# Attention on Trainium2: the product of y with the reciprocal denominators moved from GpSimd to VectorE

## The chip, the core and the metric

The kernel runs on one core of a Trainium2 chip. Its time is the device time of the execution in microseconds (us); a median of several runs is given. The engines are named as in the profile: PE (TensorE, matrix products), PEld (its weight loads), DVE (VectorE), ACT (ScalarE), POOL (GpSimd) and SP (SyncE, which here only issues DMAs).

## What is computed

One transformer layer with adaptive layer norm on 2048 tokens of width 1024. The part that matters is the attention, with 32 query heads that share 8 key and value heads:

```python
q = (x @ Wq.T).reshape(b, t, h_kv, g, d).transpose(0, 2, 3, 1, 4)   # h_kv 8, g 4, d 32
k = (x @ Wk.T).reshape(b, t, h_kv, d).transpose(0, 2, 1, 3)
v = (x @ Wv.T).reshape(b, t, h_kv, d).transpose(0, 2, 1, 3)
att = jnp.einsum('bhgqd,bhkd->bhgqk', q, k) / scale
att = jax.nn.softmax(att, axis=-1)
y = jnp.einsum('bhgqk,bhkd->bhgqd', att, v)
return y.transpose(0, 3, 1, 2, 4).reshape(b, t, e) @ Wo.T + bo
```

In front of it stand the modulation, a layer norm and the products for q, k and v; behind it the output projection and a gated feed-forward network of 2752 inner columns. All of it is in float32 or in float32 split into two parts.

## The kernel before

The program has five stages. The attention stage (`stage_attention`) works in 32 units: 8 key heads times 4 blocks of 512 queries, with the 4 query heads of the group side by side. Each unit has 16 steps, `k` = 0 to 15, one for 128 keys. The order of every engine is written out by hand, and the engines meet through semaphores alone.

In a unit `u`, PE makes for each step four transposed score tiles (128 keys x 512 queries, `scores_t`), from which ACT takes the exponentials (`pr`, eight buffers, L1057). It also makes four "turns": score tiles (128 queries x 512 keys, `turn`) of a unit ahead, from which DVE takes maxima (L1086). A unit has 64 turns. They run ahead of their unit, so that the turns 60 to 63 of unit `u + 1` are made in step 12 of unit `u`, and those of unit `u + 2` follow from step 13 on. When all 64 are there, DVE forms the row maximum (`row_max`, L1091, end of step 12), PE transposes it in step 14 (L1160), DVE writes it as two rows (`max_rows`, L1099 and L1101, between turns 5 and 6), and SP stores these into the q stack (`store_max`, L907). The first `scores_t` of the next unit waits for that store. The turns and the transposition take four PSUM banks in rotation (`score_banks`), so PE can fill a bank only when DVE is through with the fourth tile back. In even steps PE also makes the products with v for two steps at once (`by_v`, 16 products).

The softmax denominators are sums of the exponentials. POOL adds them in pairs (`pair`, L996, eight in a unit, `j` = 0 to 7), with one further sum (`quad_sum`, L1009) and four sums by accumulating DMA (`sum_by_dma`, L1005, behind the pairs 1, 3, 4 and 7). Before it issues the third of these it waits for the first two. In the next unit PE finishes the sums by products with ones in steps 2, 4 and 6 (`denominators`), ACT copies the result in step 6 (`copy_den`, L1048), and it goes the way of `den_trip` on SP's queue: out to DRAM (L916), back in spread over 128 partitions (L919), through DVE's `recip` (L1106, in step 9 behind the step's second turn), out again (L927), and back as four loads, each of which spreads one row over 32 partitions of `rden_b` (L931, `rden_loaded`). Before these loads SP waits that the product of the unit before is done (`y_done`).

The product itself is `y_out` on POOL (L1016): `yo = ysb * rden_b`, 128 x 512 float32, all three in SBUF. `ysb` is ACT's copy of the accumulated y of the last unit (L1042, step 0). In a unit `u` POOL makes it for unit `u - 1`, behind pair 5 and the quad sum (`Y_AFTER`). SP stores the result with `store_y` (L850), which stands in its queue behind `store_max`; the loads of q for a later unit (L890) follow it. DVE runs the units 0 to 30 only; unit 31 has no turns. The last unit's product is `last_division` (L882) on DVE.

Of the kernel before, what the change touches and what calls it, by code (L numbers as in the profile page):

```python
# [7 lines left out]
ALU = mybir.AluOpType  # L8
# [11 lines left out]
GH = HQ // HKV  # L20
# [633 lines left out]
def stage_attention(nc, ctx, block, qkv, wo, q_dram, k_dram, v_dram, y_dram, den_dram, kq0, qs, vg, q_loaded, v_loaded,  # L654
# [9 lines left out]
    NU = HKV * QB  # L664
# [19 lines left out]
    DEN_COPY = 6  # L684
    RECIP_AT = 9
    Y_AFTER = 5
    DW = GH * NB // P
    TSTEP = 14
    PER = NTURN // KT
# [2 lines left out]
    with ExitStack() as st:  # L692
        def sb(name, shape, dt, offset):
            return place(nc, offset, "att_" + name, shape, dt)

        def sem(name):
            return ctx.enter_context(nc.semaphore("att_" + name))
# [6 lines left out]
        rden_b = sb("rden_rows", [P, NB], F32, offs[0])  # L704
# [3 lines left out]
        mT = [sb(f"max_T_{n}", [GH * NB // P, P], F32R, offs[6 + i]) for i, n in enumerate(("hi", "lo"))]  # L708
        den_in = sb("den_spread", [P, DW], F32, offs[8])
        rden = sb("rden_spread", [P, DW], F32, offs[9])  # L710
        ysb = [sb(f"y_raw{i}", [P, NB], F32, R5 + i * 4 * NB) for i in range(2)]
        yo = [sb(f"y_out{i}", [P, NB], F32, R5 + (2 + i) * 4 * NB) for i in range(2)]
# [13 lines left out]
        y_copied, y_done, y_stored = sem("y_copied"), sem("y_done"), sem("y_stored")  # L726
        const_done = sem("consts_done")
        den_copied, den_stored, den_loaded = sem("den_copied"), sem("den_stored"), sem("den_loaded")
        rden_stored, rden_loaded = sem("rden_stored"), sem("rden_loaded")
# [29 lines left out]
        def units(eng, unit):  # L759


            for u in range(NU):
                unit(u, u % BODY, u // QB)

        def is_first(u):
            return isinstance(u, int) and u == 0
# [5 lines left out]
        def nth_turn(u, q):  # L772
            return u * NT1 + event(q)

        def nth_transpose(u):
            return (u + 1) * NT1 + (0 if beyond(u, 1) else TQ)
# [36 lines left out]
        def turn_buffer(u, q):  # L813
            return smp[of_event[nth_turn(u, q)][0]]
# [17 lines left out]
        def steps_done(u, q):  # L832

            return 2 if u == 1 and q == TQ - 1 else 1

        def beyond(u, n):

            return isinstance(u, int) and u + n >= NU
# [46 lines left out]
        def _(sp):  # L885
# [24 lines left out]
            def spread(v):  # L910
                return v.rearrange("h (a w) -> (h a) w", w=DW)

# [60 lines left out]
        @block.gpsimd  # L973
        def _(pool):
            def pair(u, j):
                pool.wait_ge(exp_done, NST + 2 * GH * (j + 1) + u * NX)

                if j == 0:
                    pool.wait_ge(den_done, 1 + u * ND)
                elif j == 1:  # L980
                    if u:
                        pool.wait_ge(quad_done, u)
                elif j == 2:
                    if u:
                        pool.wait_ge(dma_sum[3], u * 16)
                elif j == 3:
                    pool.wait_ge(den_done, 3 + u * ND)
                elif j == 4:
                    pool.wait_ge(den_done, 2 + u * ND)
                elif j == 5:  # L990
                    pool.wait_ge(dma_sum[0], 16 + u * 16)
                elif j == 6:
                    pool.wait_ge(dma_sum[1], 16 + u * 16)
                elif j == 7:
                    pool.wait_ge(dma_sum[2], 16 + u * 16)
                nc.gpsimd.tensor_tensor(ps[PAIR_SLOT[j]][:], pr[2 * j % NP][:], pr[(2 * j + 1) % NP][:],  # L996
                                        ALU.add).then_inc(pair_done, 1)

            def sum_by_dma(u, i):
                into, other = DMA_SUM[i]  # L1000
                pool.wait_ge(pair_done, NP // 2 + SUM_PAIRS[i] + 1 + u * PAIRS)
                if i == 2:
                    pool.wait_ge(dma_sum[0], 16 + u * 16)
                    pool.wait_ge(dma_sum[1], 16 + u * 16)
                pool.dma_start(ps[into][:], ps[other][:], accum_op=ALU.add).then_inc(dma_sum[i], 16)  # L1005

            def quad_sum(u):
                pool.wait_ge(pair_done, NP // 2 + 6 + u * PAIRS)
                nc.gpsimd.tensor_tensor(ps[4][:], ps[4][:], ps[1][:], ALU.add).then_inc(quad_done, 1)  # L1009

            def y_out(u, c):

                pool.wait_ge(rden_loaded, 16 * GH + u * 16 * GH)
                pool.wait_ge(y_copied, u + 1)
                pool.wait_ge(y_stored, 16 + u * 16)
                nc.gpsimd.tensor_tensor(yo[c % 2][:], ysb[c % 2][:], rden_b[:], ALU.mult).then_inc(y_done, 1)  # L1016

            def unit(u, c, g):
                if is_first(u):
                    for i in range(2):  # L1020
                        pool.wait_ge(qkv["stored"][i], qkv["all_stored"])
                for j in range(PAIRS):
                    pair(u, j)
                    if j in DMA_AFTER:
                        sum_by_dma(u, DMA_AFTER[j])
                    if j == QUAD_AFTER:
                        quad_sum(u)
                    if j == Y_AFTER and not is_first(u):
                        y_out(u - 1, c - 1)

            pool.sem_inc(pair_done, NP // 2)
            nc.gpsimd.memset(ks[1][SR:SR + 2, :].bitcast(F32), -1.0).then_inc(const_done, 1)
            pool.wait_ge(const_done, 2)
            units(pool, unit)
# [46 lines left out]
        @block.vector  # L1081
        def _(v):
            def turn(u, c, q):

                v.wait_ge(sm_ready, nth_turn(u, q) + 1)
                nc.vector.reduce_max(cmax[c % 2][:, q:q + 1], turn_buffer(u, q)[:], AX.X  # L1086
                                     ).then_inc(sm_done, steps_done(u, q))

            def row_max(u, c):
                v.wait_ge(sm_done, nth_turn(u, NTURN - 1) + 1 + NSM)  # L1090
                nc.vector.reduce_max(rmax[c % 2][:], cmax[c % 2][:].rearrange("p (r k) -> p r k", k=T // NB),  # L1091
                                     AX.X).then_inc(rmax_done, 1)

            def max_rows(u, c):

                src = transpose_buffer(u)
                v.wait_ge(sm_ready, nth_transpose(u) + 1)
                v.wait_ge(m_stored, u * 32)
                nc.vector.tensor_copy(mT[0][:], src).then_inc(mT_hi, 1)  # L1099
                v.wait_ge(mT_hi, u + 1)  # L1100
                nc.vector.tensor_tensor(mT[1][:], src, mT[0][:].bitcast(F32), ALU.subtract).then_inc(sm_done, 1)  # L1101

            def recip(u):
                v.wait_ge(den_loaded, 16 + u * 16)
                v.wait_ge(rden_stored, 16 + u * 16)
                nc.vector.reciprocal(rden[:], den_in[:]).then_inc(rden_done, 1)  # L1106

            def first_y():
                v.wait_ge(wo.y_copied, 1)
                v.wait_ge(*first_y_room)  # L1110
                v.wait_ge(pv_done, NP + (NU - 1) * KT + KT // 2 + 2)
                raw = wo.y_first[:].rearrange("p (k t) -> p k t", t=P)
                nc.vector.tensor_copy(wo.ysp[0][0], raw).then_inc(wo.y0_hi, 1)
                v.wait_ge(wo.y0_hi, 1)
                nc.vector.tensor_tensor(wo.ysp[0][1], raw, wo.ysp[0][0].bitcast(F32), ALU.subtract).then_inc(wo.y_split, 1)  # L1115

            def unit(u, c, g):
                for k in range(KT):
                    ahead = turns(u, k)
                    if k == TSTEP and not ahead and not beyond(u, 1):  # L1120
                        max_rows(u + 1, c + 1)
                    for i, (n, q) in enumerate(ahead):
                        if n == 2 and q == TQ:
                            max_rows(u + 1, c + 1)
                        turn(u + n, c + n, q)
                        if i == 1 and k == RECIP_AT and not is_first(u):
                            recip(u - 1)
                    if k == TSTEP - 2 and not beyond(u, 1):
                        row_max(u + 1, c + 1)

            nc.vector.memset(ones[:], 1.0).then_inc(const_done, 1)
            v.sem_inc(sm_done, NSM + NT1)
            v.sem_inc(rmax_done, 1)
            v.sem_inc(mT_hi, 1)
            v.sem_inc(y_done, 2)
            v.sem_inc(y_stored, 16)
            for u in range(NU - 1):
                unit(u, u % BODY, u // QB)
            recip(NU - 2)
            first_y()  # L1140
            wo.lo_of_y(v, 1)
# [1055 lines left out]
```

## Time and profile before

| what | value |
|---|---|
| median of 3 runs | 3423.8 us (3422.91 to 3424.23) |
| the profiled execution's own time | 3422.06 us |
| its span in the trace | 3420.3 us |
| granted TensorE clock, mean | 0.995 |
| busy: PE, DVE, ACT, POOL | 98%, 66%, 46%, 48% of the span |
| attention stage | from about 400 to 1965 us |

The profile is of one execution. A row of a timeline gives the start in us from the span's start, the length, the engine ("q" behind it: an instruction of its queue, a DMA's issue), the line, what is written from what, the count of instructions merged into the row, and in brackets the idle time before it with what ended it. Lines are those of the kernel before. Time to landing is counted from the start of a DMA's issue.

### The profile page before, as it was taken

The numbers are of one execution on the slowest core, as the hardware profiler recorded it, in microseconds if no ns is written. First come the engines' busy times: TensorE is split into PE (matmuls) and PEld (weight loads), VectorE is DVE, ScalarE is ACT, GpSimd is POOL, SyncE is SP. The second block draws the span as 40 slices with busy tenths as digits, with TensorE's granted clock in tenths as the row PEclk, the third lists the DMA queues.
The fourth block names the chain that finished last, engine by engine and source line by source line (L and its number), as shares of the span: only waits on it lengthen the run. The fifth ranks groups of instructions, "written<-read, shape, count | busy, mean of one in ns | idle before, by whom it ended". The sixth has DMA issues, their size and how long they took to land.

```text
span 3420.3 us, 45315 instructions
## 1 busy us (share of the span) xinstructions
PE 3362.6 (98%) x16999; PEld 2280.3 (67%) x16999; DVE 2248.2 (66%) x3760; ACT 1584.2 (46%) x2992; POOL 1638.5 (48%) x730
## 2 busy tenths in 40 slices
PE   7999999999999999999999999999999999999999
PEld 5788555555555555555555388888888888887887
DVE  6767887787777778778777288644444444444728
ACT  3211576676666666666666623222221222214544
POOL 1223789989999999899898810000000000001010
PEclk9999999999999999999999999999999999999999
DMA  6567655656565555656555555611111111004222
GB/s 240 192 203 217 161 109 114 123 109 128 107 126 112 112 120 114 126 108 126 111 108 120 134 158 180 177 31 30 31 31 31 31 31 31 24 20 152 93 74 90
DMA packets 197620, 370.35 MB, mean 108 GB/s; under 512 B 44288, under 2 KB 119552, under 8 KB 179008
## 3 DMA queue, kind: packets, MB, share of 16 engines
q0 software_dynamic: 39808, 204.24, 25.9%
q1 hardware_dynamic: 154176, 157.45, 16.4%
q10 hardware_dynamic: 3456, 6.29, 0.6%
q8 instruction: 110, 1.80, 0.2%
q14 instruction: 70, 0.57, 0.1%
HBM read 168.29 MB, written 64.87 MB: 68 GB/s over the span
## 4 chain that ended last, share of the span: by engine, by line
PE 88%; DVE 5%; DMA 3%; ACT 2%; issue 1%; SPq 0%; POOL 0%; ACTq 0%; DVEq 0%; POOLq 0%
PE att_scores L1153 15%; PE att_scores_T L1167 14%; PE att_y_acc L1178 14%; PE gu_gate_acc L1754 14%; PE gu_up_acc L1754 13%; PE wo_acc L1447 5%; PE down_acc L2087 4%; PE qkv_qk_acc L629 3%; PE att_den_acc L867 2%; PE down_acc L2118 2%; DMA qkv_wqkv_raw<-in_wmod 1%; ACT qkv_h_affine L346 1%; DVE att_chunk_max L1086 1%; DMA qkv_wmod_lo<-in_wmod 1%; PE qkv_v_acc L610 1%
## 5 line engine op out<-in xcount | busy, mean ns | idle before, releaser
L1086 DVE TENSOR_REDUCE att_chunk_max<-att_scores 128x1 f32<-128x512 f32 x1984 | 1213.0, 681 | 318.0 <-PE att_scores L1153 317.9
L1057 ACT ACTIVATE att_exp<-att_scores_T 128x512 f32<-128x512 f32 x2048 | 1036.0, 622 | 432.9 <-PE att_scores_T L1167 412.8
L996 POOL TENSOR_TENSOR att_exp_pair<-att_exp 128x2048 f32<-128x2048 f32 x256 | 1204.3, 4774 | 16.5 <-ACT att_exp L1057 9.4
L1178 PE MATMUL att_y_acc<-att_exp,att_v_head 128*32 128x512 f32 x4096 | 497.3, 603 | 0.0
L1611 POOL DMA_DIRECT2D inter_scratch<-gu_inter x84 | 45.4, 540 | 853.5 <-DVE gu_inter L1488 853.5
L1153 PE MATMUL att_scores<-att_kq,att_q_stack 96*128 96x512 f32 x768 | 314.4, 414 | 0.4 <-DVE qkv_qk_out_lo L442 0.3
L1153 PE MATMUL att_scores<-att_k_stack,att_q_stack 96*128 96x512 f32 x768 | 314.4, 412 | 0.0
L1167 PE MATMUL att_scores_T<-att_q_stack,att_k_stack 98*128 98x512 f32 x768 | 300.9, 414 | 6.3 <-DMA att_q_stack<-att_max_T_lo 3.9
L1167 PE MATMUL att_scores_T<-att_q_stack,att_kq 98*128 98x512 f32 x768 | 298.6, 408 | 2.0 <-ACT att_exp L1057 1.7
L1676 ACT ACTIVATE gu_magnitude<-gu_value 128x512 f32<-128x512 f32 (+1 forms) x88 | 55.8, 634 | 512.0 <-DVE gu_value L1712 512.0
L1178 PEld LDWEIGHTS att_y_acc<-att_exp,att_v_head 128*32 128x32 f32 x4096 | 107.3, 109 | 238.7 <-ACT att_exp L1057 151.4
L1711 DVE TENSOR_TENSOR gu_rounded<-gu_up_acc,gu_rounded 128x512 f32<-128x512 f32 x84 | 58.1, 692 | 311.8 <-PE gu_up_acc L1754 311.8
L1754 PE MATMUL gu_gate_acc<-h_hi,shared_split 128*128 128x512 f32 x704 | 224.0, 389 | 0.0
L1754 PE MATMUL gu_up_acc<-h_hi,shared_split 128*128 128x512 f32 x704 | 223.8, 389 | 0.0
L1153 PEld LDWEIGHTS att_scores<-att_kq,att_q_stack 96*128 96x128 f32 x768 | 145.9, 190 | 107.5 <-DVE att_chunk_max L1086 49.9
L1153 PEld LDWEIGHTS att_scores<-att_k_stack,att_q_stack 96*128 96x128 f32 x768 | 145.3, 189 | 104.9 <-DVE att_chunk_max L1086 43.6
L1167 PEld LDWEIGHTS att_scores_T<-att_q_stack,att_k_stack 98*128 98x128 f32 x768 | 144.1, 189 | 94.7 <-ACT att_exp L1057 62.5
L1167 PEld LDWEIGHTS att_scores_T<-att_q_stack,att_kq 98*128 98x128 f32 x768 | 145.1, 189 | 73.6 <-ACT att_exp L1057 46.4
L1005 POOL DMA_DIRECT2D att_exp_pair<-att_exp_pair x128 | 111.4, 870 | 130.9 <-DMA att_exp_pair<-att_exp_pair 98.8
L1447 PE MATMUL wo_acc<-wo_hi,shared_split 128*128 128x512 f32 x512 | 162.9, 395 | 2.7 <-DVE shared_split L1115 2.6
L1672 ACT ACTIVATE gu_sigmoid<-gu_gate_acc 128x512 f32<-128x512 f32 (+1 forms) x88 | 52.7, 598 | 220.8 <-PE gu_gate_acc L1754 220.8
L1754 PEld LDWEIGHTS gu_gate_acc<-h_hi,shared_split 128*128 128x128 f32 x704 | 132.2, 188 | 27.5
(246 smaller groups left out, 6061.4 us busy)
## 6 DMA issues: line engine op xcount, KB each, us to landing
att_exp_pair<-att_exp_pair POOLq DMA_DIRECT2D x128, 1024.0 KB, 7.3
att_q_stack<-q_scratch SPq DMA_DIRECT2D x72, 256.0 KB, 5.8
qkv_wqkv_raw<-in_wmod POOLq DMA_DIRECT2D x32, 512.0 KB, 4.6
shared_raw<-in_wd_t POOLq DMA_DIRECT2D x34, 256.0 KB, 3.0
qkv_x_tile<-in_x SPq DMA_DIRECT2D x16, 512.0 KB, 4.1
q_scratch<-qkv_qk_out_hi POOLq DMA_DIRECT2D x32, 256.0 KB, 3.7
q_scratch<-qkv_qk_out_lo POOLq DMA_DIRECT2D x32, 256.0 KB, 4.3
y_scratch<-att_y_out SPq DMA_DIRECT2D x32, 256.0 KB, 2.6
```

The costliest lines, as they stand in the source:

```text
L629: ins = nc.tensor.matmul(qkp[cc % QKB][:], w[a][:, m, k, :], hT[b % 2][z][:, k, :], start=(k == 0 and n == 0), stop=(k == FT - 1 and n == 2))
L867: ins = nc.tensor.matmul(den_buffer(u)[h * DH:(h + 1) * DH, :], ones[:], part[:, h * NB:(h + 1) * NB], start=(i == 0), stop=(i == ND - 1))
L996: nc.gpsimd.tensor_tensor(ps[PAIR_SLOT[j]][:], pr[2 * j % NP][:], pr[(2 * j + 1) % NP][:], ALU.add).then_inc(pair_done, 1)
L1005: pool.dma_start(ps[into][:], ps[other][:], accum_op=ALU.add).then_inc(dma_sum[i], 16)
L1057: nc.scalar.activation(pr[k % NP][:, h * NB:(h + 1) * NB], stp[bank_of(u, c, GH * k + h)][:], ACT.Exp, scale=INV_SQRT_DH).then_inc(exp_don ...
L1086: nc.vector.reduce_max(cmax[c % 2][:, q:q + 1], turn_buffer(u, q)[:], AX.X).then_inc(sm_done, steps_done(u, q))
L1153: nc.tensor.matmul(turn_buffer(u, q)[:], qs[c % 4][0:SR, h, qt * P:(qt + 1) * P], ks[c // QB % 2][0:SR, kc * NB:(kc + 1) * NB], start=True ...
L1167: nc.tensor.matmul(stp[bank_of(u, c, i)][:], ks[c // QB % 2][0:SR + 2, k * P:(k + 1) * P], qs[c % 4][0:SR + 2, h, :], start=True, stop=Tru ...
L1178: ins = nc.tensor.matmul(yp[h * DH:(h + 1) * DH, :], vg[c // QB % 2][:, k, :], pr[k % NP][:, h * NB:(h + 1) * NB], start=(k == 0), stop=(k ...
L1447: ins = nc.tensor.matmul(acc[t % 2][:, half * NB:(half + 1) * NB], wo.ysp[t % 2][a][:, k, :], (wo.hi, wo.lo)[z][:, half, k, :], start=(k = ...
L1754: ins = nc.tensor.matmul(dst, gu.w[j][m][a][:, k * P:(k + 1) * P], h2[z], start=(k == 0 and q == 0), stop=(k == FT - 1 and q == 2))
L2087: ins = nc.tensor.matmul(acc[t][:], lhs_a[(h * IT + k) % 2][:, t * P:(t + 1) * P], w[n][k], start=(k == 0 and n == 0), stop=(k == FULL))
```

## The change

The product of y leaves POOL's sequence in every unit but the last, where DVE has no unit of its own. DVE makes it instead, in step 12 behind the step's second turn, for the units 1 to 30 (30 products), with the same three waits and the same increment of `y_done`. Nothing else changes.

```diff
     Y_AFTER = 5
+    Y_STEP = 12
@@
-                    if j == Y_AFTER and not is_first(u):
+                    if j == Y_AFTER and u == NU - 1:
                         y_out(u - 1, c - 1)
@@
+            def y_product(u, c):
+                v.wait_ge(rden_loaded, 16 * GH + u * 16 * GH)
+                v.wait_ge(y_copied, u + 1)
+                v.wait_ge(y_stored, 16 + u * 16)
+                nc.vector.tensor_tensor(yo[c % 2][:], ysb[c % 2][:], rden_b[:], ALU.mult).then_inc(y_done, 1)
+
@@
                         if i == 1 and k == RECIP_AT and not is_first(u):
                             recip(u - 1)
+                        if i == 1 and k == Y_STEP and not is_first(u):
+                            y_product(u - 1, c - 1)
```

On DVE, from the reciprocal of a unit to the rows of maxima, the order before is:

```order
L1106 RECIPROCAL att_rden_spread<-att_den_spread 128x16
L1086 TENSOR_REDUCE att_chunk_max<-att_scores 128x1 x14
L1091 TENSOR_REDUCE att_row_max<-att_chunk_max 128x16
L1086 TENSOR_REDUCE att_chunk_max<-att_scores 128x1 x6
L1099 CAST att_max_T_hi<-att_scores 16x128
```

And now (the lines are numbered anew):

```order
L1113 RECIPROCAL att_rden_spread<-att_den_spread 128x16
L1087 TENSOR_REDUCE att_chunk_max<-att_scores 128x1 x12
L1108 TENSOR_TENSOR att_y_out<-att_y_raw,att_rden_rows 128x512
L1087 TENSOR_REDUCE att_chunk_max<-att_scores 128x1 x2
L1092 TENSOR_REDUCE att_row_max<-att_chunk_max 128x16
L1087 TENSOR_REDUCE att_chunk_max<-att_scores 128x1 x6
L1100 CAST att_max_T_hi<-att_scores 16x128
```

The product stands behind the twelfth of the fourteen maxima between the reciprocal and the row maximum; two maxima, the row maximum and six maxima of the next but one unit are behind it.

On POOL, from the second sum by DMA of a unit on, the order before is:

```order
L1005 DMA att_exp_pair<-att_exp_pair 128x2048
L996 TENSOR_TENSOR att_exp_pair<-att_exp 128x2048
L1005 DMA att_exp_pair<-att_exp_pair 128x2048
L996 TENSOR_TENSOR att_exp_pair<-att_exp 128x2048
L1009 TENSOR_TENSOR att_exp_pair<-att_exp_pair 128x2048
L1016 TENSOR_TENSOR att_y_out<-att_y_raw,att_rden_rows 128x512
L996 TENSOR_TENSOR att_exp_pair<-att_exp 128x2048 x2
```

And now:

```order
L1006 DMA att_exp_pair<-att_exp_pair 128x2048
L997 TENSOR_TENSOR att_exp_pair<-att_exp 128x2048
L1006 DMA att_exp_pair<-att_exp_pair 128x2048
L997 TENSOR_TENSOR att_exp_pair<-att_exp 128x2048
L1010 TENSOR_TENSOR att_exp_pair<-att_exp_pair 128x2048
L997 TENSOR_TENSOR att_exp_pair<-att_exp 128x2048 x2
```

The product between the quad sum and pair 6 is gone, and all else on POOL keeps its order.

## Rows read from the trace of the kernel before

**Rows 1.** The page: busy time of each engine; a costly group of weight loads.

```profile
PE 3362.6 (98%) x16999; PEld 2280.3 (67%) x16999; DVE 2248.2 (66%) x3760; ACT 1584.2 (46%) x2992; POOL 1638.5 (48%) x730
...
L1153 PEld LDWEIGHTS att_scores<-att_kq,att_q_stack 96*128 96x128 f32 x768 | 145.9, 190 | 107.5 <-DVE att_chunk_max L1086 49.9
```

**Rows 2.** Waits, attention stage, 400 to 1965 us: total, times, longest.

```profile
DVE att_chunk_max L1086 <- PE att_scores L1153: 312.0, 242, 3.0
...
PEld att_scores_T L1167 <- DMA att_q_stack<-att_max_T_lo: 7.0, 6, 2.3
...
PE att_scores_T L1167 <- DMA att_q_stack<-att_max_T_lo: 4.3, 5, 1.9
```

**Rows 3.** View of the tile of y's product: count, ns least, median, most.

```profile
L1016 POOL TENSOR_TENSOR att_y_out<-att_y_raw,att_rden_rows x31: 1272/1282/1304, 454.4 to 1964.4; 128x512 f32<-128x512 f32 x31
```

**Rows 4.** Timeline of DVE in one unit: start, us, line [idle before].

```profile
941.62 4.88 DVE L1086 TENSOR_REDUCE att_chunk_max<-att_scores 128x1 f32<-128x512 f32 x8 [0.91 <-PE att_scores L1153]
947.53 0.69 DVE L1086 TENSOR_REDUCE att_chunk_max<-att_scores 128x1 f32<-128x512 f32 x1 [1.03 <-PE att_scores L1153]
948.25 0.22 DVE L1091 TENSOR_REDUCE att_row_max<-att_chunk_max 128x16 f32<-128x64 f32 x1
948.39 3.67 DVE L1086 TENSOR_REDUCE att_chunk_max<-att_scores 128x1 f32<-128x512 f32 x6
```

**Rows 5.** Timeline of POOL in the same unit.

```profile
937.76 0.86 POOL L1005 DMA_DIRECT2D att_exp_pair<-att_exp_pair  x1 [0.30 <-POOL att_exp_pair L996]
938.61 4.63 POOL L996 TENSOR_TENSOR att_exp_pair<-att_exp 128x2048 f32<-128x2048 f32 x1
947.36 0.89 POOL L1005 DMA_DIRECT2D att_exp_pair<-att_exp_pair  x1 [4.12 <-DMA att_exp_pair<-att_exp_pair]
947.97 4.91 POOL L996 TENSOR_TENSOR att_exp_pair<-att_exp 128x2048 f32<-128x2048 f32 x1
```

**Rows 6.** Line L1352 on DVE: subtraction, both inputs in SBUF; ns.

```profile
L1352 DVE TENSOR_TENSOR wo_h_lo<-wo_h_affine,h_hi x24: 691/693/694, 2049.6 to 2179.6; 128x512 fp32r<-128x512 f32 x24
```

**Rows 7.** Tile of the row loads, 943 to 944 us: the unit's last load.

```profile
L931 SPq DMA_DIRECT2D att_rden_rows<-den_scratch x1: 1525/1525/1525, 942.6 to 942.6; - x1
...
DMA to landing us min/median/max: 5.0/5.0/5.0
```

**Rows 8.** Timeline of PE in the same unit.

```profile
948.49 0.40 PE L1153 MATMUL att_scores<-att_k_stack,att_q_stack 96*128 96x512 f32 x1
...
950.70 0.27 PE L1160 MATMUL att_scores<-ident,att_row_max 128*16 128x128 f32 x1
...
955.46 0.48 PE L1167 MATMUL att_scores_T<-att_kq,att_k_stack 98*128 98x512 f32 x1
```

**Rows 9.** Timelines of DVE and POOL, 1955 to 1985 us; line L1266, ns.

```profile
1964.71 1.23 DVE L1115 TENSOR_TENSOR shared_split<-wo_y_first,shared_split 128x1024 fp32r<-128x1024 f32 x1
1965.85 5.38 DVE L1266 TENSOR_TENSOR shared_split<-shared_raw,shared_split 128x1024 fp32r<-128x1024 f32 x1
...
1964.35 1.28 POOL L1016 TENSOR_TENSOR att_y_out<-att_y_raw,att_rden_rows 128x512 f32<-128x512 f32 x1
1965.58 10.11 POOL L996 TENSOR_TENSOR att_exp_pair<-att_exp 128x2048 f32<-128x2048 f32 x2
...
L1266 DVE TENSOR_TENSOR shared_split<-shared_raw,shared_split x15: 1216/1218/5379, 1965.8 to 2142.2; 128x1024 fp32r<-128x1024 f32 x15
```

**Rows 10.** Around 1398 us: last row load, DVE's and POOL's timelines.

```profile
L931 SPq DMA_DIRECT2D att_rden_rows<-den_scratch x1: 1252/1252/1252, 1394.3 to 1394.3; - x1
...
DMA to landing us min/median/max: 5.7/5.7/5.7
...
1394.39 4.27 DVE L1086 TENSOR_REDUCE att_chunk_max<-att_scores 128x1 f32<-128x512 f32 x7
...
1399.07 4.90 POOL L996 TENSOR_TENSOR att_exp_pair<-att_exp 128x2048 f32<-128x2048 f32 x1
```

## Prediction

> **What bounds the kernel now.** I began with the busy shares of the page: PE 98%, DVE 66%, POOL 48% [rows 1]. The change touches only the attention stage, which runs from about 400 to 1965 us in 32 units of some 50 us. There the view of waits says who is late. DVE's maxima sit idle for PE's scores, 312 us in all; PE has no wait for DVE in that list, only 4.3 us (and its weight loads 7.0) for the rows of maxima that come by DMA [rows 2]. So PE sets the time of this stage. An instruction taken off POOL or put on DVE matters only through what it makes PE wait for. Next I asked who waits for the product of y. It takes 1.28 us on POOL, 31 times, and the view of its tile names no engine that waited for it [rows 3]. Taking it away frees nothing that PE waits for.
>
> The rest is read in one unit, the one whose twelve maxima behind the reciprocal end at 945.90 us. I call the 14 maxima between the reciprocal and the row maximum m1 to m14, and the six behind it n1 to n6. m13 is the last of a row of eight that ends at 941.62 + 4.88 = 946.50; one starts every 0.60 us, so m12 ends at 945.90. Then DVE is idle for 1.03 us, since PE is in its 16 products with v, and m14 starts at 947.53 [rows 4]. That hole is where the change puts the product, in front of m13.
>
> **The change part by part.** *Removed from POOL:* 30 products of 1.28 us, 38 us, all beside PE: gain 0. POOL already has a hole of 4.12 us in each unit, in which it waits for its own DMA sum; it gets longer [rows 5]. *Added on DVE:* 30 products. No row shows this operation on DVE; the nearest is a subtraction of the same shape with both inputs in SBUF, 693 ns [rows 6]. By the overlap of neighbours (0.60 from start to start for 0.68 of duration) the next one starts 0.61 later. If the product could start at once, m13 would end 0.61 later, at 947.11, before m14 starts: cost 0. From below I exclude a gain by this term, since an engine that PE does not wait for gets more work.
>
> *The wait that comes with it.* On POOL the product stood so late (957 us) that its denominators were always there. On DVE it asks for them at 945.90. The last of the four row loads of this unit is issued at 942.6 and lands 5.0 us later, at 947.60 [rows 7]. So DVE stands 1.70 us, and queued behind the product are m13, m14, the row maximum and n1 to n6, which PE waits for: it has four score banks, so the scores for n3 need m13 done, those for n4 m14, and the transposition in step 14 needs n3 done. Worked out: product 947.62, m13 948.23 to 948.91, m14 from 948.83 in place of 947.53, so everything behind is 1.30 late. n3 ended at 948.39 + 3.67 - 3 x 0.60 = 950.26 [rows 4], now 951.56. PE made the transposition at 950.70 [rows 8]. It needs n3, some 0.05 us of release (an estimate) and a weight load of 0.19 [rows 1], so 951.80: PE loses 1.10 us. The checks for n3 (948.91 + 0.24 against 948.49) to n6 give less; the transposition decides. In general PE loses the lateness minus 0.60 us, and nothing below that. It does not win it back, as nothing in PE's row is idle; the products with v behind it only let DVE catch up.
>
> I read the same two numbers in all 30 units that get a product. The loads land 0.2 to 1.9 us after the end of m12, median about 1.1, and in one unit 3.3 us before it. The sum of the lateness above 0.60 is 14.0 us over the 30 units. That is one bound. The other comes from POOL. The row loads share the DMA engines with POOL's second sum, issued at 937.76, whose landing ends POOL's idle time at 947.36: the row loads land within 0.6 us of it in all units but two. POOL is now freer by 1.28 us, so this sum could start earlier. In about half of the units it can't, because the pairs before it start as soon as their exponentials are there (the pair at 938.61 is such a one [rows 5]: 7.3 us before the end of m12, as in 14 units); in the others it comes up to 1.1 us sooner. Taking each unit's lateness down by that slack leaves 7.3 us. I take 10 us, in the middle, as both kinds of unit will be there.
>
> *The other neighbour on SBUF.* The pairs on POOL read SBUF for 4.9 us at a time. At the end of the stage a DVE operation with two SBUF inputs met one: started at 1965.85 beside a pair, it took 5.38 us, where its 14 sisters take 1.22, and the two pairs on POOL together took 10.11, where the pairs of our unit take 4.63 and 4.91 [rows 5, 9]. So either can block the other for its whole length. An earlier one, at 1964.71 beside POOL's short product, took 1.23 and was not held up, so the rows do not agree among themselves. In our unit the next pair starts at 947.97, 0.37 after the landing: the product is there first and POOL's pair waits, which costs nothing. In the unit around 1398 us the loads land at 1394.3 + 5.7 = 1400.0, but the pair started at 1399.07 and ends at 1403.97 [rows 10]; m12 had ended one step before m13's end (1398.66), at 1398.07. There the product would start at 1403.97, 5.9 late, and PE would lose 5.3. One unit of 30 is clearly so, two more have less than 0.15 us to spare. I take one: 5.3 us; bounds 0 and three, 16 us.
>
> The Trainium skill, "SBUF — State Buffer", section "Who interferes with whom", says that a VectorE instruction with two SBUF inputs and a GpSimd instruction that reads SBUF exclude one another: the one that starts second is blocked until the first is through. The row of 5.38 us agrees, that of 1964.71 does not. By the rule alone the blocked units cost what stands above; without it that term would be 0.
>
> *SP.* The store of y now follows the two loads of row maxima at once, some 5 us sooner, and the next q load is issued as soon as the next unit has begun (955.46 [rows 8]). These move to a time when nothing waits for them: 0. The sum: 10 + 5.3 = 15 us on top of the profiled execution's 3422.06, so 3437.4; the median of the runs stands 1.7 above that execution: **3439 us**.
>
> **The rivals.** *Hidden after all.* If POOL's sum and with it the row loads come 0.5 us sooner in every unit, only 2 us are left: 3426. For it: one unit has the loads 3.3 us early because its sum was issued late, so the landing hangs on that sum alone. Against: half of the pairs are bound by the exponentials.
> *Blocked by the pairs.* The spare time between landing and pair is 0.37 us in our unit and 0.4 in the median. If the landings slip by some tenths against the pairs, DVE stands for a whole pair. The point is where the product's start passes the pair's (947.97); each such unit costs 5.3 us. Ten units give 53 + 10: 3487; five more than forecast give 3439 + 27 = 3466.
> *Later rows of maxima.* The y store (256 KB) right behind the rows of maxima may delay their landing, on which PE's next unit waits; each 0.3 us costs 9 us: 3448. For it: PE already waits 4.3 us for these rows [rows 2].
> *Faster.* The same traffic, moved, may end those waits. With nothing lost on DVE, and both kinds of wait gone (4.3 and 7.0 us), the time would be 3423.8 - 11.3 = 3412.5; with half of that 3418. Against: the change moves nothing that those rows wait behind.
> That the change doesn't do what it says is excluded by the order of instructions.
>
> **How the numbers follow.** Forecast 0.53; hidden 0.22; blocked in many units 0.12; later rows 0.08; faster 0.05. Faster or slower means by over 0.2%, 6.8 us, about what a measurement can tell from no change, so from 3430.6 up. Of the forecast's share 0.05 lies below that (lateness 7, no unit blocked). Slower 0.48 + 0.12 + 0.08 = 0.68, same 0.22 + 0.05 = 0.27, faster 0.05. The range begins at 3425, within the hidden case, and ends at 3466 with six blocked units; it leaves out the faster case, a sliver of the hidden one and most of the blocked one.
>
> **What would show it.** In the trace of the changed kernel: the product on DVE 30 times at about 0.69 us; idle time of DVE in front of it put down to the row loads, some 25 to 35 us in all; PE waiting for DVE's maxima in the attention stage, some 10 us; one or two products of about 5 us. Many products near 5 us mean the blocked rival. Idle time under 0.6 us each and no wait of PE mean the hidden one. If rows of maxima land later than 1.9 us after issue more often than now, it is the third. I would be wrong at the root if PE lost time where DVE is not late.

## The result

| | before | changed |
|---|---|---|
| median of 6 runs | 3424.02 us (3422.91 to 3427.5) | 3588.82 us (3581.93 to 3598.03) |
| ratio to before, 95% interval | | 1.0482 (1.047 to 1.0495) |
| span of the profiled execution | 3420.3 us | 3581.7 us |

The change costs 165 us. The forecast was 3439 us with a range up to 3466; its sign was right, but it had 15 us of loss where 165 came.

The page of the changed kernel, the rows that answer to [rows 1] and [rows 3]:

```profile
PE 3428.5 (96%) x16999; PEld 2314.3 (65%) x16999; DVE 2385.2 (67%) x3790; ACT 1594.0 (45%) x2992; POOL 1603.6 (45%) x700
...
L1108 DVE TENSOR_TENSOR att_y_out<-att_y_raw,att_rden_rows 128x512 f32<-128x512 f32 x30 | 137.8, 4593 | 22.8 <-DMA att_rden_rows<-den_scratch 22.8
```

The 30 products do not take 0.69 us on DVE but 4.6 in the mean. The view of the tile shows that they come in two kinds, with the least at 691 ns and the median at 5586:

```profile
L1108 DVE TENSOR_TENSOR att_y_out<-att_y_raw,att_rden_rows x30: 691/5586/5836, 449.1 to 2067.2; 128x512 f32<-128x512 f32 x30
```

Read one by one in the timeline, 24 take 4.4 to 5.8 us and 6 take 0.69. The waits of the attention stage (400 to 2150 us), against [rows 2]:

```profile
PE att_scores L1162 <- DVE att_chunk_max L1087: 99.5, 24, 5.8
...
DVE att_y_out L1108 <- DMA att_rden_rows<-den_scratch: 22.8, 30, 2.2
...
PE att_scores_T L1176 <- DMA att_q_stack<-att_max_T_lo: 1.1, 2, 0.8
```

PE now waits for DVE's maxima 24 times, once for each long product, 99.5 us in all. That is not the whole of 165. The view of windows, with busy time by engine and the granted clock of PE, gives the rest. First the changed kernel's attention stage, then that of before:

```profile
405.00:2130.00 1725.00, 1618.05 (x8672) 836.30 (x8669) 1333.32 (x2068) 1062.53 (x2063) 1395.45 (x406) 0.95 0.51 107
```

```profile
405.00:1968.00 1563.00, 1551.79 (x8652) 800.47 (x8651) 1191.99 (x2032) 1049.42 (x2058) 1424.58 (x435) 1.00 0.57 117
```

The stage is 162 us longer. PE is not busy for 1725 - 1618 = 107 us, where it was 11: 96 more. And PE is busy 66 us longer with the same matrix products, at a mean granted clock of 0.95 in place of 1.00. So 96 + 66 = 162, or 4.0 + 2.8 us for each of the 24 units. By the trace's clock records PE is busy for 136 us of this stage at a granted clock of 0.50, where it was 12; at half pace these 124 us more cost 62 of the 66.

One such unit, first DVE, then POOL, then PE:

```profile
1117.42 5.60 DVE L1108 TENSOR_TENSOR att_y_out<-att_y_raw,att_rden_rows 128x512 f32<-128x512 f32 x1 [0.36 <-DMA att_rden_rows<-den_scratch]
1122.94 1.28 DVE L1087 TENSOR_REDUCE att_chunk_max<-att_scores 128x1 f32<-128x512 f32 x2
```

```profile
1117.03 0.87 POOL L1006 DMA_DIRECT2D att_exp_pair<-att_exp_pair  x1 [2.69 <-DMA att_exp_pair<-att_exp_pair]
1117.64 4.82 POOL L997 TENSOR_TENSOR att_exp_pair<-att_exp 128x2048 f32<-128x2048 f32 x1
1122.54 4.89 POOL L1010 TENSOR_TENSOR att_exp_pair<-att_exp_pair 128x2048 f32<-128x2048 f32 x1
```

```profile
1119.42 0.39 PE L1176 MATMUL att_scores_T<-att_q_stack,att_k_stack 98*128 98x512 f32 x1
1123.67 0.50 PE L1162 MATMUL att_scores<-att_k_stack,att_q_stack 96*128 96x512 f32 x1 [3.86 <-DVE att_chunk_max L1087]
```

The product's recorded start (1117.42) is 0.22 us ahead of the pair's (1117.64). Yet it ends at 1123.02, which is 0.56 us behind the pair's end: it did its work only when the pair was through. PE stands for 3.86 us. What its granted clock does behind that is in the windows of the same unit (the column in front of the last two):

```profile
1119.00:1123.00 4.00, 0.81 (x4) 0.34 (x2) 4.00 (x2) 1.50 (x3) 3.92 (x2) 1.00 1.12 227
1123.00:1125.00 2.00, 1.33 (x4) 0.93 (x5) 1.97 (x6) 0.56 (x1) 2.00 (x1) 0.82 0.03 4
1125.00:1131.00 6.00, 6.00 (x24) 2.24 (x22) 3.52 (x8) 2.31 (x5) 6.00 (x2) 0.50 0.03 11
1131.00:1136.00 5.00, 5.00 (x25) 3.14 (x25) 4.21 (x8) 3.85 (x8) 2.03 (x2) 0.99 0.27 66
```

Behind the stand the granted clock is 0.50 (1.2 in place of 2.4 GHz) for 6.8 us, and 24 matrix products fill 6 us.

Six products are of the other kind. That of the unit around 507 us starts just ahead of POOL's DMA issue and is over in 0.69:

```profile
507.29 0.69 DVE L1108 TENSOR_TENSOR att_y_out<-att_y_raw,att_rden_rows 128x512 f32<-128x512 f32 x1 [1.43 <-DMA att_rden_rows<-den_scratch]
```

```profile
507.30 0.87 POOL L1006 DMA_DIRECT2D att_exp_pair<-att_exp_pair  x1 [4.16 <-DMA att_exp_pair<-att_exp_pair]
507.90 4.89 POOL L997 TENSOR_TENSOR att_exp_pair<-att_exp 128x2048 f32<-128x2048 f32 x1
```

Over all 30 units the lag of the product's start behind the start of that DMA issue tells the kinds apart, not its place against the pair's recorded start. The six short ones start 0.36 ahead to 0.04 behind the issue. The long ones start 0.13 or more behind it, 22 of them ahead of the pair's recorded start and two inside the pair.

### The profile page after: what moved, and what is told of

Its sections match the earlier page's. It is cut to its first block, busy times and chain, and to the rows that moved or that the text cites. A ratio compares the mean times of both kernels' runs of the same rounds, so it can differ in the third digit from the quotient of the medians.

```text
span 3581.7 us, 45315 instructions
## 1 busy us (share of the span) xinstructions
PE 3428.5 (96%) x16999; PEld 2314.3 (65%) x16999; DVE 2385.2 (67%) x3790; ACT 1594.0 (45%) x2992; POOL 1603.6 (45%) x700
## 4 chain that ended last, share of the span: by engine, by line
PE 78%; DVE 10%; DMA 7%; SPq 2%; ACT 2%; issue 1%; POOL 0%; ACTq 0%; DVEq 0%; POOLq 0%
PE gu_gate_acc L1763 13%; PE gu_up_acc L1763 13%; PE att_scores L1162 12%; PE att_scores_T L1176 11%; PE att_y_acc L1187 11%; PE wo_acc L1456 5%; PE down_acc L2096 4%; DVE att_y_out L1108 4%; DMA att_rden_rows<-den_scratch 3%; PE qkv_qk_acc L629 3%; PE att_den_acc L868 2%; PE down_acc L2127 2%; SPq L932 2%; DVE att_chunk_max L1087 2%; DMA qkv_wqkv_raw<-in_wmod 1%
## 5 line engine op out<-in xcount | busy, mean ns | idle before, releaser
L997 POOL TENSOR_TENSOR att_exp_pair<-att_exp 128x2048 f32<-128x2048 f32 x256 | 1190.8, 4665 | 208.4 <-ACT att_exp L1058 114.1
L1187 PE MATMUL att_y_acc<-att_exp,att_v_head 128*32 128x512 f32 x4096 | 509.6, 616 | 0.0
L1162 PE MATMUL att_scores<-att_kq,att_q_stack 96*128 96x512 f32 x768 | 323.9, 427 | 37.9 <-DVE att_chunk_max L1087 37.5
L1162 PE MATMUL att_scores<-att_k_stack,att_q_stack 96*128 96x512 f32 x768 | 324.0, 424 | 37.8 <-DVE att_chunk_max L1087 37.8
L1176 PE MATMUL att_scores_T<-att_q_stack,att_k_stack 98*128 98x512 f32 x768 | 308.7, 425 | 3.5 <-ACT att_exp L1058 2.4
L1176 PE MATMUL att_scores_T<-att_q_stack,att_kq 98*128 98x512 f32 x768 | 308.3, 421 | 1.4 <-ACT att_exp L1058 1.4
L1010 POOL TENSOR_TENSOR att_exp_pair<-att_exp_pair 128x2048 f32<-128x2048 f32 x32 | 153.9, 4809 | 2.5
L1108 DVE TENSOR_TENSOR att_y_out<-att_y_raw,att_rden_rows 128x512 f32<-128x512 f32 x30 | 137.8, 4593 | 22.8 <-DMA att_rden_rows<-den_scratch 22.8
```

What stands on the lines that cost most here:

```text
L1108: nc.vector.tensor_tensor(yo[c % 2][:], ysb[c % 2][:], rden_b[:], ALU.mult).then_inc(y_done, 1)
L1162: nc.tensor.matmul(turn_buffer(u, q)[:], qs[c % 4][0:SR, h, qt * P:(qt + 1) * P], ks[c // QB % 2][0:SR, kc * NB:(kc + 1) * NB], start=True ...
L1176: nc.tensor.matmul(stp[bank_of(u, c, i)][:], ks[c // QB % 2][0:SR + 2, k * P:(k + 1) * P], qs[c % 4][0:SR + 2, h, :], start=True, stop=Tru ...
L1187: ins = nc.tensor.matmul(yp[h * DH:(h + 1) * DH, :], vg[c // QB % 2][:, k, :], pr[k % NP][:, h * NB:(h + 1) * NB], start=(k == 0), stop=(k ...
```

## The experiments

Theory A: a DVE operation with two SBUF inputs and POOL's operations exclude each other, and POOL gets the way in earlier than the trace's start of its pair says. Theory B: something else draws the product out, such as the loads or the wait. Theory C: all of the loss comes to PE as DVE's lateness, with the halved clock behind it. Rival D: POOL, held up, carries a good part. Each time is a median beside that of before on the same chip.

### The second input in PSUM

```diff
             def y_product(u, c):
+                ahead = u + 1 + 1
+                v.wait_ge(sm_ready, nth_turn(ahead, NTURN - 2) + 1)
...
-                nc.vector.tensor_tensor(yo[c % 2][:], ysb[c % 2][:], rden_b[:], ALU.mult).then_inc(y_done, 1)
+                nc.vector.tensor_tensor(yo[c % 2][:], ysb[c % 2][:], turn_buffer(ahead, NTURN - 2)[:], ALU.mult
+                                        ).then_inc(y_done, 1)
```

> Edit: the product on DVE stays where it is and waits for the same things, but its second input is the score tile of the 13th maximum, which lies in PSUM, in place of the reciprocal denominators in SBUF (so y is wrong; nothing is left out of the time). Theory A (two SBUF inputs on DVE and POOL's operations exclude each other): all 30 products take 0.69 us, no clock drop, and only the lateness of the row loads remains, so 3426 to 3438 us. Theory B (something else draws the product out: the loads that still write, or the wait itself): the products stay near 5.6 us and the time near 3589 us.

Measured: 3423.7 us against 3422.81, ratio 1.0002 (0.9993 to 1.0012). The view of the tile:

```profile
L1110 DVE TENSOR_TENSOR att_y_out<-att_y_raw,att_scores x30: 686/689/690, 444.7 to 1906.3; 128x512 f32<-128x512 f32 x30
```

All 30 take 0.69 us, with the same waits and one more (for the score tile) at the same place, and with the pair of most units starting 0.1 to 0.7 us behind them as in the changed kernel. The loss is gone with the second SBUF input, so theory B falls. The time is even under the 3426 us expected: what the lateness costs is too small to see here (the interval of the ratio ends at 1.0012, that is 4 us).

### The wait alone

```diff
             def y_product(u, c):
                 v.wait_ge(rden_loaded, 16 * GH + u * 16 * GH)
                 v.wait_ge(y_copied, u + 1)
                 v.wait_ge(y_stored, 16 + u * 16)
-                nc.vector.tensor_tensor(yo[c % 2][:], ysb[c % 2][:], rden_b[:], ALU.mult).then_inc(y_done, 1)
```

with the product back on POOL in every unit.

> Edit: DVE waits for the row loads at the same place in step 12, but makes nothing; the product is on POOL as before. It prices the lateness alone, without the product's 0.61 us. By the prediction's rule PE loses the lateness minus 1.2 us here (0.6 for the rule, 0.6 for the missing product), so at most some 4 us in all: 3424 to 3429 us. Rival: the wait itself carries a good part of the 165 us (then over 3450).

Measured: 3423.11 us, ratio 0.9999 (0.999 to 1.0009). DVE waits, and PE hardly does:

```profile
DVE att_chunk_max L1087 <- DMA att_rden_rows<-den_scratch: 30.0, 29, 2.3
...
PE att_scores L1161 <- DVE att_chunk_max L1087: 0.5, 2, 0.3
```

Behind thirty microseconds of idle DVE, PE waits 0.5 for its maxima. The wait that the change adds costs nothing that these runs can tell from zero.

### The pair waits for the product, the DMA issue does not

```diff
                 elif j == 5:
                     pool.wait_ge(dma_sum[0], 16 + u * 16)
+                    if 0 < u < NU - 1:
+                        pool.wait_ge(y_done, 2 + u)
```

> Edit: POOL's pair 5 waits for DVE's product (units 1 to 30), while the DMA issue ahead of that pair does not. It takes the pair away as a neighbour and leaves the DMA issue. Theory A1 (the DMA issue on POOL takes the port and hands it to the pair): a product that starts behind the issue's start is held for what is left of the issue, so it takes 0.7 to 1.2 us; the time is 3426 to 3445 us. Theory A2 (the pair gets the port although the product began first; the issue plays no part): all products take 0.69 us, time 3426 to 3438 us. Theory B (no part of it is due to the pair): products stay near 5.6 us, time near 3589 us.

Measured: 3424.94 us, ratio 1.0002 (0.9992 to 1.0012). Tile and waits:

```profile
L1110 DVE TENSOR_TENSOR att_y_out<-att_y_raw,att_rden_rows x30: 691/693/693, 448.0 to 1908.8; 128x512 f32<-128x512 f32 x30
```

```profile
POOL att_exp_pair L999 <- DVE att_y_out L1110: 7.8, 20, 0.7
...
PE att_scores L1164 <- DVE att_chunk_max L1089: 1.1, 2, 0.8
```

This is the changed kernel with its two SBUF inputs and one wait more on POOL, of 7.8 us in all, and the 165 us are gone. The DMA issue, which began 0.1 to 0.7 us ahead of most products, holds nothing up by itself: not one takes 0.7 to 1.2 us. So it is the pair that has to be there, but A1 as I had put it (the issue takes the way in) and A2 (the issue plays no part) are not told apart by this run.

### Meetings of two operations, each engine released with a chosen lag

A kernel of its own: ACT releases one engine, makes a copy of chosen width, and releases the other. DVE multiplies 128x512, POOL adds 128x2048, and no data is shared.

> A kernel of its own that leaves the whole computation out: only DVE operations of 128x512 set against POOL operations with a chosen lag, each trial twice. Theory A1: a DVE operation with two SBUF inputs that starts 0.2 to 0.5 us ahead of a POOL pair (4.6 us), with no DMA issue before it, runs its 0.69 us and the pair gets longer; with a DMA issue on POOL begun ahead of it, it waits for the pair's end (over 5 us). Theory A2: also without the DMA issue a pair that starts within the first 0.5 us of the DVE operation holds it up for its whole length. In both, an operation with one input in PSUM, and a maximum, take 0.69 us at any time, and the one that starts within a pair waits for its end.

The timeline, with POOL's pair begun ahead of DVE's operation, and then (second fence) DVE begun ahead of the pair; last a DVE operation of 2048 columns:

```profile
61.39 4.49 POOL L82 TENSOR_TENSOR pool_c<-pool_a,pool_b 128x2048 f32<-128x2048 f32 x1 [0.85 <-ACT act_b L101]
61.81 4.62 DVE L61 TENSOR_TENSOR dve_c<-dve_a,dve_b 128x512 f32<-128x512 f32 x1 [0.72 <-ACT act_c L102]
```

```profile
31.60 0.69 DVE L61 TENSOR_TENSOR dve_c<-dve_a,dve_b 128x512 f32<-128x512 f32 x1 [4.61 <-ACT act_b L101]
32.00 4.64 POOL L82 TENSOR_TENSOR pool_c<-pool_a,pool_b 128x2048 f32<-128x2048 f32 x1 [0.66 <-ACT act_c L102]
...
42.20 2.29 DVE L63 TENSOR_TENSOR dve_c<-dve_a,dve_b 128x2048 f32<-128x2048 f32 x1 [4.61 <-ACT act_b L101]
42.34 6.51 POOL L82 TENSOR_TENSOR pool_c<-pool_a,pool_b 128x2048 f32<-128x2048 f32 x1 [0.40 <-ACT act_c L102]
```

Where the pair is first, DVE's operation ends 0.55 us behind the pair's end (61.39 + 4.49 = 65.88; 66.43). Where DVE is first, by 0.13 to 0.51 us, it takes 0.69 in all ten trials and the pair waits; behind the long operation it takes 6.51 in place of 4.49. So without a DMA issue the recorded starts tell who goes first, and A2 falls. With one input in PSUM, 0.05 and 0.42 us inside the pair, the operation takes 0.69. In this kernel no trial with a DMA issue and a pair had the issue ahead of the operation, since POOL still waited for the DMA before; the case that matters was left for the next.

### A pair queued right behind a DMA issue

The same with the trials lined up anew: the issue 0.7 us ahead to 0.7 behind the operation.

> A kernel of its own that leaves the whole computation out: DVE's 128x512 operation with two SBUF inputs against a DMA issue on POOL with a pair right behind it, at lags from the operation ahead of the issue to the operation behind it; also the issue alone, the issue with a pair that waits for the operation, and an operation with one input in PSUM. Theory A1, sharpened by the first such kernel (there the issue alone held nothing up, and a pair without an issue ahead of it lost against an operation that had begun): a pair queued behind the issue holds the port before its own recorded start, from about the issue's start on; so an operation that starts 0.1 us or more behind the issue's start lasts until 0.55 us after the pair's end (4.5 to 5.7 us), and one that starts ahead of the issue takes 0.69. With the pair gated or with PSUM: 0.69 always. Theory A3 (the order of the recorded starts of operation and pair decides, and something else in the full kernel made the difference): every operation that starts before the pair takes 0.69 us.

Three trials of the timeline, in which ACT's copy grows by 64 columns each:

```profile
46.33 0.87 POOL L74 DMA_DIRECT2D dma_a<-dma_b  x1 [2.09 <-ACT act_b L102]
46.37 0.69 DVE L55 TENSOR_TENSOR dve_c<-dve_a,dve_b 128x512 f32<-128x512 f32 x1 [6.86 <-ACT act_c L103]
46.94 4.79 POOL L78 TENSOR_TENSOR pool_c<-pool_a,pool_b 128x2048 f32<-128x2048 f32 x1
...
53.80 0.87 POOL L74 DMA_DIRECT2D dma_a<-dma_b  x1 [2.07 <-ACT act_b L102]
53.89 0.69 DVE L55 TENSOR_TENSOR dve_c<-dve_a,dve_b 128x512 f32<-128x512 f32 x1 [6.83 <-ACT act_c L103]
54.41 4.79 POOL L78 TENSOR_TENSOR pool_c<-pool_a,pool_b 128x2048 f32<-128x2048 f32 x1
...
61.26 0.87 POOL L74 DMA_DIRECT2D dma_a<-dma_b  x1 [2.06 <-ACT act_b L102]
61.40 5.82 DVE L55 TENSOR_TENSOR dve_c<-dve_a,dve_b 128x512 f32<-128x512 f32 x1 [6.82 <-ACT act_c L103]
61.87 4.79 POOL L78 TENSOR_TENSOR pool_c<-pool_a,pool_b 128x2048 f32<-128x2048 f32 x1
```

0.09 us behind the issue's start the operation is free; 0.14 behind it, and still 0.47 ahead of the pair's recorded start, it takes 5.82. All 12 trials with a lag of 0.14 to 0.68 are long (5.3 to 5.8), all 20 with a smaller one or none are short, and the second pass repeats the lengths of the first to 0.01 us. The other three kinds, the pair gated behind the operation (lag 0.29), the issue alone (0.14), and one input in PSUM (0.30):

```profile
182.15 0.88 POOL L74 DMA_DIRECT2D dma_a<-dma_b  x1 [2.08 <-ACT act_b L102]
182.44 0.69 DVE L55 TENSOR_TENSOR dve_c<-dve_a,dve_b 128x512 f32<-128x512 f32 x1 [7.08 <-ACT act_c L103]
183.22 4.48 POOL L78 TENSOR_TENSOR pool_c<-pool_a,pool_b 128x2048 f32<-128x2048 f32 x1 [0.19 <-DVE dve_c L55]
```

```profile
152.22 0.86 POOL L74 DMA_DIRECT2D dma_a<-dma_b  x1 [6.62 <-ACT act_b L102]
152.36 0.69 DVE L55 TENSOR_TENSOR dve_c<-dve_a,dve_b 128x512 f32<-128x512 f32 x1 [6.95 <-ACT act_c L103]
```

```profile
197.18 0.87 POOL L74 DMA_DIRECT2D dma_a<-dma_b  x1 [2.11 <-ACT act_b L102]
197.48 0.69 DVE L59 TENSOR_TENSOR dve_c<-dve_a,psum_a 128x512 f32<-128x512 f32 x1 [7.15 <-ACT act_c L103]
197.79 4.79 POOL L78 TENSOR_TENSOR pool_c<-pool_a,pool_b 128x2048 f32<-128x2048 f32 x1
```

This is A1 in its sharpened form, and A3 falls. A POOL operation that is free to go and stands right behind a DMA issue keeps the operation on DVE out from about 0.1 us behind the issue's start, that is 0.5 us before its own recorded start. What POOL does in that half microsecond the trace does not show.

### Lateness without a meeting

The product is on POOL as before; DVE waits at the same place and then makes 8, or 4, further maxima.

```diff
             def y_product(u, c):
                 v.wait_ge(rden_loaded, 16 * GH + u * 16 * GH)
-                v.wait_ge(y_copied, u + 1)
-                v.wait_ge(y_stored, 16 + u * 16)
-                nc.vector.tensor_tensor(yo[c % 2][:], ysb[c % 2][:], rden_b[:], ALU.mult).then_inc(y_done, 1)
+                v.wait_ge(sm_ready, nth_turn(u + 2, NTURN - 2) + 1)
+                for n in range(MORE):
+                    nc.vector.reduce_max(more[:, n:n + 1], turn_buffer(u + 2, NTURN - 2)[:], AX.X)
```

> Edit: the product stays on POOL as before; DVE waits at the same place in step 12 and then makes 8 further maxima of the 13th score tile (4.8 us, one input, in PSUM) in place of the blocked product. No meeting with POOL. Theory C (the 165 us are DVE's lateness, which PE waits out, plus the halved TensorE clock that follows; the port only makes the lateness): each of the 30 units loses about 4.7 us of waiting and some 2 to 3 us of halved clock, so 3424 + 30 x 7 = 3630 us, 3580 to 3650. Rival D (POOL, held up or out of step, carries a good part of the loss): clearly less per unit than the changed kernel's 6.7, below 3540 us.

> Edit: as the one with eight maxima, but four (2.4 us). It asks whether the loss is in proportion or whether the clock comes with long waits only. By the rule of the prediction PE loses the lateness (2.4 + 0.75) minus 0.6 to 0.8, some 2.4 us in each of 30 units: 3424 + 72 = 3496 us without a halved clock. With the halved clock after each, 2 to 3 us more in each unit: about 3570 us.

Measured, with two runs of each: 3597.16 us with eight (ratio 1.0497, 1.0466 to 1.0527) and 3477.57 with four (1.0148, 1.0118 to 1.0177), against 3427.43. The windows of the attention stage, eight and then four:

```profile
405.00:2140.00 1735.00, 1622.96 (x8652) 833.29 (x8650) 1335.63 (x2275) 1062.48 (x2061) 1419.80 (x434) 0.95 0.50 106
```

```profile
405.00:2020.00 1615.00, 1576.51 (x8650) 801.41 (x8648) 1261.15 (x2155) 1054.71 (x2059) 1421.45 (x434) 0.99 0.55 114
```

With eight, PE is not busy 112 us (101 more than before) and busy 71 longer; with four, 38 us (27 more) and 25 longer. Busy at a granted clock of 0.50 it is for 154 us with eight and 30 with four, so the halved clock accounts for all of the 71, but only for 9 of the 25; what the other 16 are is not shown. Eight maxima of 0.6 us make DVE about as late as a held product does, and they rebuild the whole loss, both its parts and the mean clock of 0.95, with POOL undisturbed. That is theory C; rival D asked for less than 3540. The loss is 5.7 us for each of 30 units here, and 6.8 for each of 24 in the changed kernel, whose held products make DVE somewhat later (PE mostly stands 3.9 us there and 3.2 here). Four maxima came out below both of my numbers, 50 us and not 72. My slip there: the rule subtracts 0.6 from the lateness of a product that itself takes 0.6; without the product it must subtract 1.2. Then it gives (2.4 + 0.75 - 1.2) x 30 = 58. The halved clock comes here too, but in nine stretches only, all but one of 3.4 us, and the kernel before has four such in the last 155 us of the stage. Six of the nine lie at stands of PE of 1.5 to 2.6 us; the many stands of 0.8 us have none. So it is not tied to every stand; the 29 stands here are of 1.1 us in the mean.

## Why the prediction was wrong

*What bounds the kernel, and the gain of the removal.* Right. PE sets the time; POOL lost 38 us of work and nothing became faster. In the changed kernel, where PE is late, POOL's pairs wait for exponentials, 105.7 us in all.

*The wait.* The size of DVE's idle time in front of the product was nearly right: 22.8 us where it said "25 to 35". Its price was too high: 10 us forecast, about 1 measured. The runs with one input in PSUM and with the gated pair both stand at 1.0002, which leaves room for 4 us at most, and the units of the latter sum to 0.8 us more than before (below). The mechanism is there. In the run with the gated pair a unit whose loads came 1.4 us late lasted 50.65 us, and one with 2.2 us 51.41, where an undisturbed one takes 50.0; so PE loses the lateness minus 0.8, not minus 0.6. But most loads landed only 0.4 us late, since POOL's second sum went out sooner. And PE waited less for the rows of maxima than in [rows 2], in that run 1.6 us in place of 4.3. From the first transposed score of one unit to that of the next, the 30 units sum to 1509.4 us there against 1508.6 before.

*The neighbour on SBUF.* This step failed. It said: "In our unit the next pair starts at 947.97, 0.37 after the landing: the product is there first and POOL's pair waits, which costs nothing." From that it counted one blocked unit of 30. The rule of exclusion was right, as [rows 9] had shown it in both directions, and the first of the two small kernels repeats it. What was wrong is whose start counts. The pair stood right behind a DMA issue, and there it keeps DVE out 0.5 us before its recorded start; in all units but six the product fell into that half microsecond or behind it. Had I asked for a spare time of 0.5 us in the trace of before, I would have counted 14 units of 30. (Read again, the median there is 0.53 us, not the 0.4 that I gave, and besides the blocked unit only one has less than 0.15, not two; the next has 0.18.) The others came with the change itself: POOL, 1.28 us ahead, issues its sums as soon as the exponentials allow, and with the second sum landing sooner the issue and the pair behind it moved up against the row loads. In the trace of before the product could have started 0.1 us behind that issue in the median; in the changed kernel it starts 0.4 behind it. So the pair's recorded start is only some 0.2 us behind the product's in most units. The rival "blocked by the pairs" named mechanism and turning point, but put that point at the pair's recorded start (947.97) when it is 0.5 us earlier, and with 0.12 had too small a chance.

The row that seemed to speak against exclusion, DVE's operation at 1964.71 beside POOL's short product [rows 9], was misread. The prediction counts it among the operations with two SBUF inputs. Its first input, `wo_y_first`, is a tile in PSUM (`self.y_first = bank(nc, 6, "wo_y_first", 2 * NB)` in the kernel), so it has one SBUF input, like the product of the first run and the trials with `psum_a`, which took 0.69 us beside a pair. An operation with two SBUF inputs begun 0.05 or 0.42 us inside such a short POOL operation in the small kernel was held up until 0.55 us behind its end. So the rows did agree among themselves, and my doubt in the rule had no ground.

The Trainium skill, "SBUF — State Buffer", section "Who interferes with whom", gives the shared way in to whichever instruction issues first, for its whole length. The trials without a DMA issue agree, with the recorded start taken for that moment (0.69 us where DVE is first, and until the pair's end where POOL is). With a DMA issue ahead of the pair the recorded start cannot be taken for it: by the recorded starts 2 of the 30 products would be held, and 24 were.

*The price of a blocked unit.* Forecast 5.3 us, measured 6.8. The waiting is 4.0 of it. The other 2.8 come, all but 0.2, from the halved clock, which the working did not hold at all: it took PE's pace behind a wait for granted. Together: 24 x 6.8 = 162 us where the sum had 1 x 5.3.

*SP.* The earlier store of y did no harm to the rows of maxima; PE's wait for them fell from 4.3 us to 1.1 in the changed kernel. The rival of later rows is refuted, and that of a faster kernel had a true part of a few microseconds, too small to see.

No version tried is faster than before. The one with the gated pair is equal to it (1.0002): the product's place does not matter to PE as long as nobody is held up.

## What to carry to other kernels

Before an elementwise operation with two SBUF inputs moves to VectorE, look at what GpSimd runs at that moment: 0.7 us of work lasted up to 5.8 us here, beside a GpSimd operation of 4.8, and everything queued behind it on VectorE was late by the difference. A margin read from the two recorded starts is not enough where a DMA issue stands ahead of GpSimd's operation; a wait of GpSimd's operation on VectorE's (7.8 us of idle GpSimd here) or one input in PSUM took the whole 165 us away. And where PE is the bound, add to a stand of PE of some 4 us what the halved clock costs behind it, here 0.7 us for each 1 us of waiting; with stands of about 1 us it cost far less.

## What the runs showed of the hardware that I had not expected

- A GpSimd operation of 4.8 us queued right behind a DMA issue of 0.87 us kept VectorE's operation with two SBUF inputs out from a lag of 0.14 us behind the issue's start (at 0.09 it was free), though its own recorded start is 0.61 behind the issue's. Without the issue ahead of it, it lost even against an operation begun 0.13 us before it.
- The DMA issue alone, at lags of 0.14 to 0.51 us, held up nothing (0.69 us).
- A held VectorE operation ended 0.55 to 0.56 us behind the end of GpSimd's, whatever its own start, and it got in between two GpSimd operations in a row; the second of these then took 4.93 us in place of 4.49.
- A copy from SBUF to SBUF on VectorE, with only one input, was held up as well: 4.73 us beside a pair, while a maximum over a tile of that size in SBUF took 0.69.
- At each of PE's 24 stands of some 4 us the granted clock went to 0.50 (1.2 GHz), beginning in the stand or up to 0.7 us behind its end, for 6.8 us in 20 cases and 3.4 in 4, though PE was busy without a gap from the stand's end on.
